# Second cross attention: all key chunks of the tail projected first, maximum products after the weighting, the reciprocal's step thinned

## The reference

```
SCALE = DH ** (-0.5)                       # DH = 64, H = 16
q = (x @ Wq).reshape(b, n, H, DH)          # n = 1024 tokens
k = (context @ Wk * SCALE).reshape(b, m, H, DH)   # m = 6404 keys
v = (context @ Wv).reshape(b, m, H, DH)
scores = jnp.einsum('bihd,bjhd->bhij', q, k)
attn = jax.nn.softmax(scores, axis=-1)
out = jnp.einsum('bhij,bjhd->bihd', attn, v).reshape(b, n, H * DH)
return out @ Wo + bo
```

## Time and profile before

| | us |
|---|---|
| median of 3 runs | 5598.53 (5596.75 to 5602.74) |
| profiled execution, its own time | 5582.32 |
| its span, first to last instruction | 5580.0 |
| granted clock of PE, mean over the span | 0.897 |
| heads 0 to 15 of this stage | 2923.8 to 5446.6 of the span |

### The profile page before, as it was taken

One profiled execution on the slowest core, in us unless ns is written; L12 is line 12 of the kernel. 1 busy time (PEld: TensorE's weight loads), 2 busy tenths in 40 slices (PEclk: granted clock), 3 DMA queues, 4 the chain that ended last, 5 costly groups with the idle time before them and its releaser, 6 DMA issues. The chain is left out here.

```text
span 5580.0 us, 68492 instructions
## 1 busy us (share of the span) xinstructions
PE 4551.0 (82%) x21823; PEld 2232.3 (40%) x21823; DVE 2846.9 (51%) x3426; ACT 2558.4 (46%) x4400; POOL 2765.0 (50%) x1598
## 2 busy tenths in 40 slices
PE   6898676777677777769869998999999999999883
PEld 2333343434343443423334444444444444444431
DVE  3666464736364646535654444444444444444505
ACT  1444463636363645415525545445444444444540
POOL 0000453525352535300008777777777777777790
PEclk6777798989898999957869999999999999999996
DMA  0000000000000000000010000000000000000000
GB/s 16 3 2 0 31 12 10 12 10 1 21 1 21 1 19 2 1 10 1 1 29 2 1 3 3 3 3 1 4 1 3 3 3 3 1 4 1 1 1 8
DMA packets 18027, 34.97 MB, mean 6 GB/s; under 512 B 3418, under 2 KB 12250, under 8 KB 16746
## 3 DMA queue, kind: packets, MB, share of 16 engines
q1 hardware_dynamic: 17642, 30.22, 1.7%
HBM read 29.69 MB, written 0.52 MB: 5 GB/s over the span
## 5 line engine op out<-in xcount | busy, mean ns | idle before, releaser
L1160 POOL TENSOR_TENSOR xat_p_sum<-xat_p_sum,xat_p_full 128x1024 f32<-128x1024 f32 x768 | 1823.4, 2374 | 527.9 <-ACT xat_p_full L1110 497.1
L1110 ACT ACTIVATE xat_p_full<-xat_sc 128x512 f32<-128x512 f32 (+1 forms) x1632 | 870.1, 594 | 978.0 <-PE xat_sc L1020 943.7
L1202 DVE TENSOR_REDUCE xat_part<-xat_ring 128x2 f32<-128x1024 f32 (+1 forms) x832 | 950.2, 1181 | 579.5 <-PE xat_ring L980 570.9
L1006 PE MATMUL xat_acc<-xat_p_full,xat_v 128*64 128x512 f32 (+1 forms) x3264 | 807.8, 615 | 0.0
L1019 PE MATMUL xat_sc<-xat_q_hh,xat_k_hl 128*128 128x512 f32 (+1 forms) x1632 | 779.0, 477 | 14.9 <-ACT xat_p_full L1110 13.5
L1020 PE MATMUL xat_sc<-xat_q_lm,xat_k_h 128*128 128x512 f32 (+1 forms) x1632 | 645.1, 395 | 0.0
L978 PE MATMUL xat_ring<-xat_k_hl,xat_q_hh 64*128 64x512 f32 (+1 forms) x832 | 382.7, 490 | 231.0 <-DVE xat_k_hl L1199 205.4
L1697 POOL TENSOR_TENSOR loc_weights_n<-loc_probs,loc_rinv 128x512 f32<-128x512 f32 (+1 forms) x384 | 303.3, 810 | 458.6 <-DVE loc_rinv L1793 305.0
L1019 PEld LDWEIGHTS xat_sc<-xat_q_hh,xat_k_hl 128*128 128x128 f32 (+1 forms) x1632 | 303.9, 186 | 416.9 <-issue 252.7
L1681 POOL TENSOR_TENSOR loc_sind<-loc_qk,loc_tab 128x512 f32<-128x512 f32 x192 | 238.6, 1265 | 453.8 <-DVE loc_ss L1737 453.8
L1476 PE MATMUL loc_pr<-loc_w_qkv,loc_xs 128*128 128x512 f32 x576 | 364.0, 766 | 102.4 <-DVE loc_cosd L1744 56.4
(11 more groups left out here) (393 smaller groups left out, 7171.7 us busy)
## 6 DMA issues: line engine op xcount, KB each, us to landing
loc_w_qkv<-in_L_ffn_w SPq DMA_DIRECT2D x6, 1536.0 KB, 7.3
loc_w_o<-in_L_ffn_wo SPq DMA_DIRECT2D x6, 512.0 KB, 3.2
xat_ctxT<-in_ctxT SPq DMA_DIRECT2D x12, 256.0 KB, 2.7
xat_w_qk<-in_L_xattn_wqk SPq DMA_DIRECT2D x16, 128.0 KB, 2.0
loc_w<-in_L_ffn_w SPq DMA_DIRECT2D x6, 341.0 KB, 2.9
loc_w<-in_L_ffn_w SPq DMA_DIRECT2D x6, 192.0 KB, 2.3
loc_rope<-in_rope SPq DMA_DIRECT2D x1, 1024.0 KB
xat_w_o<-in_L_xattn_wo SPq DMA_DIRECT2D x16, 64.0 KB, 1.8
```

The lines of the kernel that those rows point to most:

```text
L1006: last = pe.matmul(acc[h * GROUP:(h + 1) * GROUP, :], v[0:size, t, e * GROUP:(e + 1) * GROUP], p_full[0:size, (e * NT + t) % RING, cols(h) ...
L1110: act.activation(p_full[0:size, at_.buffer(t), cols(h)], sc[0:size, n % 3, :], ACT.Exp, scale=GROUP ** -0.5).then_inc(S["exp_done"], 1)
L1160: pool.tensor_tensor(p_sum[:, e, :], first_in, p_full[:, at_.buffer(t), :], ALU.add)\
L1202: ins = dve.tensor_reduce(part[:, 2 * t:2 * t + 2, c], ring[:, b, :, 0:chunks[c][1]], AX.X, ALU.max)
```

## The change

The items are laid into the steps by other rules; not one is added or removed. The chunks come in the order 11, 12, 0, 1, ..., 10, with K of 11 in step 0, of 12 in step 1, and the others where they were. M run from step 1 to step 24: two in a step, behind the weighting; the third of steps 7 to 12 stands in `mid`. Steps 4 and 6 have one M each. U moves to `post` of step 4, whose one M stands in `mid`; Y moves to `post` of step 6, behind its M.

```
-    order = [OWN, 0, OWN + 1, *range(1, OWN)]
+    order = [*range(OWN, NCH), *range(OWN)]
...
-                steps[3 if sums else 1][post] += [("U", 0, 0)]
-                steps[5 if sums else 4][post] += [("Y", 0, 0)]
+                steps[4 if sums else 1][post] += [("U", 0, 0)]
...
-                for c in order:
-                    steps[1 + 2 * (c - OWN) if c >= OWN else 2 * c + 2][pre] += [("K", c, 0)]
-                for n in range(NCH * NTOK // 2):
-                    step = steps[2 + n * (NJ - 3) // (NCH * NTOK // 2)]
-                    step[mid if len(step[mid]) < 2 else post] += [("M", order[n // 4], n % 4)]
+                for n, c in enumerate(order):
+                    steps[n if c >= OWN else 2 * c + 2][pre] += [("K", c, 0)]
+                maxima = [("M", c, m) for c in order for m in range(NTOK // 2)]
+                for j in range(1, NJ - 1):
+                    here = {4: 1, 6: 1}.get(j, 2) if j <= 6 else -(-len(maxima) // (NJ - 1 - j))
+                    for k in range(here):
+                        steps[j][mid if j == 4 or k >= 2 else post] += [maxima.pop(0)]
...
+            if ends:
+                steps[6 if sums else 4][post] += [("Y", 0, 0)]
```

More of the change, by code:

```diff
@@ L780, in __init__ @@
             if ends:
-                steps[3 if sums else 1][post] += [("U", 0, 0)]
-                steps[5 if sums else 4][post] += [("Y", 0, 0)]
+                steps[4 if sums else 1][post] += [("U", 0, 0)]
             if fills and sums:
                 steps[0][pre] += [("Q", 0, 0)]
-                for c in order:
-                    steps[1 + 2 * (c - OWN) if c >= OWN else 2 * c + 2][pre] += [("K", c, 0)]
-                for n in range(NCH * NTOK // 2):
-                    step = steps[2 + n * (NJ - 3) // (NCH * NTOK // 2)]
-                    step[mid if len(step[mid]) < 2 else post] += [("M", order[n // 4], n % 4)]
-                steps[NJ - 1][post] += [("T", 0, 0)]
+                for n, c in enumerate(order):
[5 more added lines that the diff above has]
+                        steps[j][mid if j == 4 or k >= 2 else post] += [maxima.pop(0)]
+                assert not maxima
+                steps[NJ - 1][post] += [("T", 0, 0)]
+            if ends:
+                steps[6 if sums else 4][post] += [("Y", 0, 0)]
+            if fills and sums:
+                where = {item: (j, k) for j, step in enumerate(steps) for k, items in enumerate(step) for item in items}
+                for n, c in enumerate(order):
+                    assert where["K", c, 0] < where["M", c, 0]
+                    assert n + 3 >= NCH or where["M", c, NTOK // 2 - 1] < where["K", order[n + 3], 0]
             elif fills:
```

## The result

Four runs of the changed kernel have a median of 5327.8 us (5318.6 to 5332.1), four of the kernel before 5597.6 us: a ratio of 0.9516, with a 95% interval of 0.9499 to 0.9532. The time saved is 270 us, against 206 forecast.

What follows compares the result with a forecast made beforehand. PE was taken to set the pace, leaving its waits to remove: 229 + 8 + 18 = 255 us go, 26 + 20 + 3 come, saving 206. From 5598.5 us that gave a forecast of 5393 us, range 5345 to 5445.

Steps and rivals of the forecast that it cites:

- The stalls: In steps with a K, PE's second M waits for DVE's low part of K; all 173 waits go, saving 229 us.
- Reciprocal and clock: Around step 4, M's waits for DVE's reciprocal go, 8 us, and the clock's fall after them, 18 us.
- Term (1): On PE, M behind the weighting costs more than M ahead of it: 26 us lost, ends 0 and 52.
- Term (2): Steps 8, 10, 12: second M behind the weighting waits for DVE to free the `mid` M's buffer; 20 us lost, ends 0 and 58.
- Terms (3) and (4): Head's start: K in step 0 delays ACT, 3 us lost, ends 0 and 15. Head's end: later last M costs T nothing.
- A: Stalls keep their size at the second M behind the weighting; about 5602 us, no change; chance 0.04.
- C: Clock falls at the weighting of each step with a K, 239 us come; 5632 us, slower; chance 0.03.
- B: POOL becomes the bound in steps without K and V, losing 18 us; 5411 us; chance 0.05.
- D: Whole gain: the costs of M's place, DVE waits and head's start are near nothing; 5344, about 5350 us; chance 0.13.

Runs made afterwards that it cites:

- mid_all: Changed kernel with the first two M of a step put back ahead of the weighting (third behind); ratio 0.9898 to the kernel before.
- m_only: Kernel before with only M moved: first two of a step behind the weighting, third ahead, U and Y behind M; ratio 0.9582 to the kernel before.
- k_first: mid_all with K issued at its step's start and copied by ACT ahead of the step's Exps; ratio 0.9750 to the kernel before.
- Mid_odd: Changed kernel with the pair of M ahead of the weighting in odd steps from 3 on; ratio 0.9560 to the kernel before.
- split: Changed kernel with each two-M step's pair parted, one M ahead of the weighting and one behind; ratio 0.9648 to the kernel before.
- thirds_odd: Changed kernel with the third M moved from steps 7 to 12 to odd steps 7 to 17; ratio 0.9483 to the kernel before, 0.9507 when repeated.
- u_at_3: Changed kernel with U back in step 3 and Y in step 5, both behind M; ratio 0.9572 to the kernel before.
- after_again: The changed kernel run once more, unaltered; ratio 0.9538 to the kernel before.

## Why the prediction was right or wrong

**The stalls.** Right in mechanism and number; mid_all, m_only and k_first show it from three sides. The size was low by 0.10 each. I had measured from M to M (1.62 in place of 0.34), but the stall also splits the pair: behind it, the lone second M takes 0.43 to the weighting (3045.18 to 3045.61 in the earlier trace rows) and not 0.33. The steps' lengths say 1.38 = 6.83 - 5.45. That is 173 x 0.10 = 17 us more gain.

**Reciprocal and clock.** Right. The wait for the reciprocal is gone, and behind U the changed kernel runs as worked out, on PE and on DVE (head 1):
```profile
3093.55 1.03 PE L1000 MATMUL xat_ring<-xat_p_sum,xat_ones 128*64 128x512 f32 x4
...
3097.46 1.94 PE L1015 MATMUL xat_acc<-xat_p_full,xat_v 128*64 128x512 f32 x8
3099.32 0.38 PE L987 MATMUL xat_ring<-xat_k_hl,xat_q_hh 64*128 64x260 f32 x1
```
```profile
3094.62 3.36 DVE L1217 RECIPROCAL xat_inv<-xat_ring 128x512 f32<-128x512 f32 x1 [0.87 <-PE xat_ring L1000]
3098.11 1.33 DVE L1230 TENSOR_TENSOR xat_o<-xat_o_raw,xat_inv 128x512 f32<-128x512 f32 x1
3099.75 1.83 DVE L1211 TENSOR_REDUCE xat_part<-xat_ring 128x2 f32<-128x520 f32 x2 [0.31 <-PE xat_ring L989]
```
DVE is done 5.89 us after U (5.9 forecast) and then waits 0.31 for M. The weighting takes 1.94 in place of 2.98, in every head. Counted afresh, what it took above 1.94 before is 16 us in all, for my 18.

**Term (1), M dearer behind the weighting: 26 us.** This step failed, and it is the largest part of the miss, 23 to 26 us. I took the 0.43 that one lone M takes to the next scores for the price of M's last place behind a weighting, and put it under every pair. It is the price of standing alone. Mid_odd shows the side to be worth nothing in itself and split shows 0.20 a group. The number of groups hardly changes (29 in a head before, besides the ones that stalls split, and 30 after, 15 x 0.20 = 3 us), so the term is 0 to 3 us. Its lower end, "the pair closes up", was the truth. The rule of the Trainium skill (TensorEngine Tiling, Key Properties), that a change of tiling mode drains the engine, had given 1 to 2 us: my rows had told two cases apart, a lone M behind and a pair ahead, that differed in two things at once, and the rule named the one that counted.

**Term (2), waits for DVE in steps with three M: 20 us.** Right in place, and 16 us in size; thirds_odd gave 16 to 19 of it back. My check for it, a row of some 45 waits, would have missed it: the row has 16 waits and 3.7 us.

**The wait for V, which the sum put at nothing.** Before, 70 pairs in odd heads waited for V's buffer at 0.14 us each, 10 us; after, no pair stands between a V and the weighting. The prediction has no term for it, because my row for a pair ahead is from head 0, where no V stands in the step, and because this wait is not listed in the record.

**Terms (3) and (4).** Step 0 is longer by some 0.4 to 0.6 us to its first weighting and the stalls at the start are gone: with 3 us for (3) I was within what can be told. No new wait of T came (one of 2.2 us, at the end of head 0's preparation, stands beside one of 1.9 before).

**The sum.** With these sizes, 246 (stalls) + 8 (reciprocal) + 16 (clock) + 10 (V) - 3 (term 1) - 16 (term 2) = 261 us. Measured in heads 0 to 14: 264, so 3 us stay without a place, no more than one kernel differs from itself. Of the 58 us by which the gain in this stage exceeds the 206, term (1) is 23, the size of a stall 17, V 10, term (2) 4. In the profiled executions the gain was 256, because the stages ahead took 6 us longer in that of after. And 15 of the 65 us come from the scale: before's profiled execution lies 16.2 below the median I forecast from, that of after 1.4 below its own, so carrying 16.2 over to the changed kernel brought in the scatter of the stages ahead. From profiled to profiled execution the miss is 50 us.

**The rivals.** A (waits move), C (slower by the clock) did not occur. POOL was not the bound (B): head 15 has the same 131.6 us, and an even head with 139.1 has POOL busy for 119.6. D, the whole gain, was the case: its 5344 still held the stall at 1.28. I had given it 0.13 and closed the range at it, though it was what the sum gave if the doubtful terms were nothing.

## What to carry to other kernels

A stall on a buffer goes when enough independent work stands between its producer and its second user; what k_first shows is that the way it is done matters (the users put behind four products: the wait all gone; the producer moved: half of the cost of a stall back, mostly as waits for another engine). Price a switch between tile shapes by the group and not by the side or the instruction, and if the only row for it is of a lone instruction, keep zero among the likely values. Read what waits cost from step to step, since in these traces waits up to 0.25 us were not listed in the record at all.

## What the runs showed that I had not expected

A wait of M for a DVE reduction that delays M by 0.25 us (0.59 in place of 0.34) is not listed as a wait in the record, and one of 0.32 is listed with 0.15. ACT's copy of V, which delays M by some 0.03 and splits the pair for another 0.10, is not listed either.

Inside a head the clock fell to 0.50 only in the kernel before, in 11 heads, after waits of 0.53 and 1.68 us that end 2.2 us apart. In u_at_3 the same 0.53 and then 0.73, 8 us apart, did not make it fall, nor did the 1.11 us at every K of mid_all. A single wait of about 2 us did it now and then: in every kernel Q waits at the start of six heads, 1.6 to 2.4 us, for DVE. Two of these in the changed kernel:
```profile
3920.51 1.98 PE L965 MATMUL xat_ring<-all_xT,xat_w_qk 128*128 128x512 f32 x4 [2.04 <-DVE xat_q_lm L1214]
...
4205.17 3.61 PE L965 MATMUL xat_ring<-all_xT,xat_w_qk 128*128 128x512 f32 x4 [2.00 <-DVE xat_q_lm L1214]
```
Behind the second the clock reads 0.50 (4206 to 4208), and Q takes 3.61 us in place of 1.98. It happened at one of the six waits in after, two in after_again, four in mid_all and none in before, split, u_at_3 and thirds_odd. So a wait of this length can be followed by the lower clock and mostly is not; what decides, and whether the 1.68 us alone would have been enough at step 4, is open.

Executions of one and the same kernel vary by 20 us and more (thirds_odd 5292.9 to 5320.3), while the changed stage varies by 3 between the two profiled executions of a kernel. For the changed kernel these took 5326.4 and 5306.2 us, and head 0 starts at 2930.2 and 2906.5: that difference lies in the stages ahead.
